# A kept score as two parts on two engines, and all sums on GpSimd, in the third feed-forward of a decoder stack

## The reference

```python
xn = _rmsnorm(x, norm_w)
q = (xn @ w_q.T).reshape(b, t, H, 2, DK)                    # H = 8 heads
sim1 = jnp.einsum('bthd,hkd->bthk', q[..., 0, :], keys[:, :, 0, :])   # 32 keys each
sim2 = jnp.einsum('bthd,hkd->bthk', q[..., 1, :], keys[:, :, 1, :])
s1, i1 = jax.lax.top_k(sim1, K)                             # K = 8
s2, i2 = jax.lax.top_k(sim2, K)
all_sc = (s1[..., :, None] + s2[..., None, :]).reshape(b, t, H, K * K)
fs, pk = jax.lax.top_k(all_sc, K)
...
hidden = jax.nn.gelu(jnp.einsum('btd,bthkd->bthk', xn, wd), approximate=False)
hidden = hidden * jax.nn.relu(fs)
return jnp.einsum('bthk,bthkd->btd', hidden, wu)
```

## Time and profile before

| | us |
|---|---|
| median of 3 runs | 3284.03 (3282.2 to 3285.31) |
| the profiled execution, its own time | 3292.13 |
| its span in the profile | 3290.0 |
| TensorE busy | 2657.0 (81%) |
| VectorE busy | 1842.7 (56%) |
| ScalarE busy | 1231.2 (37%) |
| GpSimd busy | 518.4 (16%) |

### The profile page before, as it was taken

One profiled execution on the slowest core, in us unless ns is written; L12 is line 12 of the kernel. 1 busy time (PEld: TensorE's weight loads), 2 busy tenths in 40 slices (PEclk: granted clock), 3 DMA queues, 4 the chain that ended last, 5 costly groups with the idle time before them and its releaser, 6 DMA issues.

```text
span 3290.0 us, 38345 instructions
## 1 busy us (share of the span) xinstructions
PE 2657.0 (81%) x13038; PEld 1292.2 (39%) x13089; DVE 1842.7 (56%) x4787; ACT 1231.2 (37%) x3064; POOL 518.4 (16%) x801
## 2 busy tenths in 40 slices
PE   6798898779987667888878988987899776678885
PEld 2233335334543543234423333452345335432353
DVE  5434438535655888624464444475257469875154
ACT  2545622453233101564334555224522231025741
POOL 1220001220112442000012200012201125410000
PEclk9988898889878778878769888898899687878776
DMA  4000000000100000000100000000001000000000
GB/s 164 2 1 1 1 1 25 25 2 20 33 13 0 0 26 26 1 1 30 36 8 2 1 1 1 1 25 26 1 20 33 13 1 0 26 27 1 1 1 7
DMA packets 16418, 49.52 MB, mean 15 GB/s; under 512 B 1761, under 2 KB 8801, under 8 KB 14434
## 3 DMA queue, kind: packets, MB, share of 16 engines
q1 hardware_dynamic: 15650, 45.79, 4.0%
q10 hardware_dynamic: 576, 1.29, 0.1%
HBM read 45.43 MB, written 1.05 MB: 14 GB/s over the span
## 4 chain that ended last, share of the span: by engine, by line
PE 60%; DVE 20%; ACT 9%; issue 7%; SPq 1%; POOL 1%; DMA 1%; ACTq 0%; DVEq 0%; POOLq 0%
PE psum L564 5%; PE psum L975 4%; PE psum L534 3%; DVE keep_s L2229 3%; PE psum L554 3%; PE psum L986 3%; PE psum L1510 2%; PE psum L1340 2%; PE psum L959 2%; PE psum L726 2%; DVE fs_v_s L2091 2%; ACT PT_s L630 2%; DVE mx_s L693 2%; PE psum L1802 2%; PE psum L801 2%
## 5 line engine op out<-in xcount | busy, mean ns | idle before, releaser
L630 ACT ACTIVATE PT_s<-psum 128x512 f32<-128x512 f32 (+3 forms) x768 | 342.3, 498 | 248.7 <-PE psum L554 246.0
L690 DVE CUSTOM_DVE_ANT_0 rest_s<-psum,packed_early 128x128 f32<-128x128 f32 (+3 forms) x512 | 226.6, 487 | 167.0 <-PE psum L540 164.8
L2134 PE MATMUL psum<-packed_early,keep_s 128*128 128x128 f32 x1024 | 177.7, 332 | 131.7 <-DVE keep_s L2229 131.4
L396 POOL TENSOR_SCALAR ve<-mv 128x4 f32<-128x4 f32 x48 | 14.4, 301 | 1691.0 <-DVE mv L386 1690.8
L554 PE MATMUL psum<-QS_s,KS_s 64*128 64x512 bf16 (+3 forms) x768 | 200.9, 366 | 55.8 <-DMA QS_s<-nmT_s 39.3
L540 PE MATMUL psum<-KS_s,QS_s 64*128 64x512 bf16 (+3 forms) x768 | 190.0, 364 | 54.0 <-DVE mx_s L693 29.4
L2091 POOL TENSOR_TENSOR buffer<-sim_s 128x1024 f32<-128x1024 f32 x80 | 187.3, 2353 | 240.6 <-DVE keep_s L2229 238.4
L564 PE MATMUL psum<-PT_s,vaug 128*9 128x512 f32 (+3 forms) x1536 | 183.5, 553 | 45.1 <-POOL PT_s L663 28.1
L2134 PEld LDWEIGHTS psum<-packed_early,keep_s 128*128 128x128 f32 x1024 | 147.4, 172 | 168.0 <-DVE keep_s L2229 155.9
L663 POOL TENSOR_SCALAR_AFFINE_SELECT PT_s<-PT_s 128x128 f32<-128x128 f32 x512 | 145.0, 293 | 387.7 <-ACT PT_s L630 382.8
L693 DVE TENSOR_REDUCE mx_s<-psum 128x1 f32<-128x512 f32 x256 | 160.5, 683 | 72.5 <-PE psum L540 72.1
(11 more groups left out here) (444 smaller groups left out, 5250.9 us busy)
## 6 DMA issues: line engine op xcount, KB each, us to landing
buffer<-packed_experts SPq DMA_DIRECT2D x36, 384.0 KB, 3.3
...
QS_s<-nmT_s SPq DMA_DIRECT2D x72, 8.0 KB
```

The lines of the kernel that those rows point to most:

```text
L630: a.activation(PT[:, u // 4 % 2, i, q0_of(c):T], bank[u % 3][:, q0_of(c):T], ACT.Exp, scale=scale).then_inc(exp_done.sem, 1)
L690: v.tensor_tensor_reduce(junk[:, u % 2, 0:w], bank[n % 4][:, 0:w], s.w["causal"][:, T - w:T], 1.0, -3e38, ALU.add, ALU.max, mx[:, j, h:h + ...
L2134: mm = pe.matmul(CT[:, c * P:(c + 1) * P], keep[:, n % KEPT, c * P:(c + 1) * P], s.w["ident"][:], is_transpose=True, start=(h == 0 and c % ...
```

## The change

A kept score is now written as two parts that add up to it: relu(sum - limit), made by ScalarE (L2194 of the changed kernel, into above), and limit x (sum >= limit), made by VectorE (`floored`, L2234 there, into floor) with one tensor_scalar that reads the limit twice as a pointer scalar. VectorE also makes the negated limits once a block (below, L2226 there), which ScalarE adds as a bias. TensorE transposes both parts into the same sums, 16 transposes a head instead of 8. GpSimd makes the sums of all eight heads (L2161 there), and VectorE none. above and floor have two buffers each (KEPT = 2) where keep had four. A buffer of sums is free when both parts have read it (risen, marked); the transposes wait for both parts as well.

```diff
-    KEPT, ON_POOL = 4, (0, 2, 4, 6, 7)
-    ON_DVE = tuple(h for h in range(NH) if h not in ON_POOL)
+    KEPT = 2
...
-                pe.wait_ge(*kept(n + 1))
+                pe.wait_ge(*risen(n + 1))
+                pe.wait_ge(*marked(n + 1))
...
-                for c in range(EC):
-                    mm = pe.matmul(CT[:, c * P:(c + 1) * P], keep[:, n % KEPT, c * P:(c + 1) * P], s.w["ident"][:], is_transpose=True,
-                                   start=(h == 0 and c % 4 == 0), stop=(h == NH - 1), skip_group_check=True)
+                for i, rows in enumerate((above, floor)):
+                    for c in range(EC):
+                        mm = pe.matmul(CT[:, c * P:(c + 1) * P], rows[:, n % KEPT, c * P:(c + 1) * P], s.w["ident"][:], is_transpose=True,
+                                       start=(h == 0 and i == 0 and c % 4 == 0), stop=(h == NH - 1 and i == 1), skip_group_check=True)
...
-            for i, h in enumerate(ON_POOL):
+            for h in range(NH):
                 yield max(13.0, at(j, h) - 3.0)
-                if i == 0:
+                if h == 0:
                     g.wait_ge(*sim_copied(j + 1))
-                n = j * len(ON_POOL) + i
+                n = j * NH + h
                 if n >= 2:
-                    m = n - 2
-                    g.wait_ge(*kept((m // len(ON_POOL)) * NH + ON_POOL[m % len(ON_POOL)] + 1))
-                sums(g, fs_g[:, n % 2], j, h).then_inc(sum_g.sem, 1)
+                    g.wait_ge(*risen(n - 1))
+                    g.wait_ge(*marked(n - 1))
+                m = sim[:, j % 2, h]
+                g.tensor_tensor(fs[:, n % 2], m[:, 0, :].unsqueeze(2).to_broadcast([P, NK, NK]),
+                                m[:, 1, :].unsqueeze(1).to_broadcast([P, NK, NK]), ALU.add).then_inc(summed.sem, 1)
...
+        for j in range(TJ):
+            for h in range(NH):
+                n = j * NH + h
+                yield at(j, h) + 0.4
+                total, ready = sum_of(n)
+                a.wait_ge(*ready)
+                if h == 0:
+                    a.wait_ge(*limits_ready(j + 1))
+                if n >= KEPT:
+                    a.wait_ge(*added(n - KEPT + 1))
+                a.activation(above[:, n % KEPT, :], total, ACT.Relu, bias=below[:, j % 2, h:h + 1]).then_inc(risen.sem, 1)
...
+            v.tensor_scalar(below[:, j % 2, :], thr[:, j % 2, :], -1.0, None, ALU.mult).then_inc(limits_ready.sem, 1)
...
             if n >= KEPT:
                 v.wait_ge(*added(n - KEPT + 1))
-            fs = fs.rearrange("p a b -> p (a b)")
-            v.scalar_tensor_tensor(keep[:, n % KEPT, :], fs, thr[:, j % 2, h:h + 1], fs, ALU.is_ge, ALU.mult).then_inc(kept.sem, 1)
+            v.tensor_scalar(floor[:, n % KEPT, :], total, thr[:, j % 2, h:h + 1], thr[:, j % 2, h:h + 1], ALU.is_ge, ALU.mult).then_inc(marked.sem, 1)
```

More of the change, by code:

```diff
@@ L2062, in l2_ffn @@
     N = TJ * NH
-    (chain, squares_ready, eps_added, inv_ready, xs_ready, xs_turned, xnT_ready, hidden_ready, gelu_ready, sim_ready, sim_copied, sum_v, sum_g,
-     kept, added, weighted, out_ready) = s.signals(
-        chain=1 + 4 * TJ, squares_ready=1, eps_added=1, inv_ready=1, xs_ready=TJ, xs_turned=1, xnT_ready=1, hidden_ready=EC, gelu_ready=EC,
-        sim_ready=TJ, sim_copied=TJ, sum_v=TJ * len(ON_DVE), sum_g=TJ * len(ON_POOL), kept=N, added=N, weighted=TJ, out_ready=TJ)
+    (chain, limits_ready, squares_ready, eps_added, inv_ready, xs_ready, xs_turned, xnT_ready, hidden_ready, gelu_ready, sim_ready, sim_copied, summed,
+     risen, marked, added, weighted, out_ready) = s.signals(
+        chain=1 + 4 * TJ, limits_ready=TJ, squares_ready=1, eps_added=1, inv_ready=1, xs_ready=TJ, xs_turned=1, xnT_ready=1, hidden_ready=EC, gelu_ready=EC,
+        sim_ready=TJ, sim_copied=TJ, summed=N, risen=N, marked=N, added=N, weighted=TJ, out_ready=TJ)
     s.new_stage()
@@ L2076, in l2_ffn @@
     thr = s.tile("thr9", [P, 2, NH])
-    fs_v = s.tile("fs_v9", [P, NK, NK])
-    fs_g = s.buffer[:, 2048:4096].rearrange("p (i a b) -> p i a b", i=2, a=NK)
-    keep = s.tile("keep9", [P, KEPT, NK * NK])
+    below = s.tile("below9", [P, 2, NH])
+    fs = s.buffer[:, 2048:4096].rearrange("p (i a b) -> p i a b", i=2, a=NK)
+    above = s.tile("above9", [P, KEPT, NK * NK])
+    floor = s.tile("floor9", [P, KEPT, NK * NK])
     cand = sq[:].rearrange("p j d -> p (j d)").rearrange("p (h a b) -> p h a b", h=NH, a=8)
@@ L2087, in at, with sum_of @@
         return T1 + D1 * (j * NH + h)
-    def sums(eng, dst, j, h):
-        m = sim[:, j % 2, h]
-        return eng.tensor_tensor(dst, m[:, 0, :].unsqueeze(2).to_broadcast([P, NK, NK]),
-                                 m[:, 1, :].unsqueeze(1).to_broadcast([P, NK, NK]), ALU.add)
+    def sum_of(n):
+        return fs[:, n % 2].rearrange("p a b -> p (a b)"), summed(n + 1)
     def tensor(pe):
@@ L2168, in copy_sim @@
             if j >= 2:
-                a.wait_ge(*kept(NH * (j - 1)))
+                a.wait_ge(*risen(NH * (j - 1)))
+                a.wait_ge(*marked(NH * (j - 1)))
             a.copy(sim[:, j % 2].rearrange("p h s n -> p (h s n)"), bank[2]).then_inc(sim_copied.sem, 1)
@@ L2179, in scalar @@
             a.activation(hid[:, c, :], bank[c % 2], ACT.Gelu).then_inc(gelu_ready.sem, 1)
-        for j in range(2, TJ):
-            yield at(j - 1, 1) + 3.0
-            copy_sim(j)
+        for j in range(TJ):
[9 more added lines that the diff above has]
+                a.activation(above[:, n % KEPT, :], total, ACT.Relu, bias=below[:, j % 2, h:h + 1]).then_inc(risen.sem, 1)
+                if h == 1 and 1 <= j < TJ - 1:
+                    yield at(j, h) + 3.0
+                    copy_sim(j + 1)
     def vector(v):
@@ L2210, in thresholds, with floored @@
             link(v.tensor_scalar(thr[:, j % 2, :], best[:, :, 7], 0.0, None, ALU.max))
-        def filtered(j, h):
+            v.tensor_scalar(below[:, j % 2, :], thr[:, j % 2, :], -1.0, None, ALU.mult).then_inc(limits_ready.sem, 1)
+        def floored(j, h):
             n = j * NH + h
-            if h in ON_DVE:
-                i = j * len(ON_DVE) + ON_DVE.index(h)
-                if i >= 1:
-                    before = i - 1
-                    v.wait_ge(*kept((before // len(ON_DVE)) * NH + ON_DVE[before % len(ON_DVE)] + 1))
-                sums(v, fs_v[:], j, h).then_inc(sum_v.sem, 1)
-                v.wait_ge(*sum_v(i + 1))
-                fs = fs_v[:]
-            else:
-                i = j * len(ON_POOL) + ON_POOL.index(h)
-                v.wait_ge(*sum_g(i + 1))
-                fs = fs_g[:, i % 2]
+            total, ready = sum_of(n)
+            v.wait_ge(*ready)
             if n >= KEPT:
                 v.wait_ge(*added(n - KEPT + 1))
-            fs = fs.rearrange("p a b -> p (a b)")
-            v.scalar_tensor_tensor(keep[:, n % KEPT, :], fs, thr[:, j % 2, h:h + 1], fs, ALU.is_ge, ALU.mult).then_inc(kept.sem, 1)
+            v.tensor_scalar(floor[:, n % KEPT, :], total, thr[:, j % 2, h:h + 1], thr[:, j % 2, h:h + 1], ALU.is_ge, ALU.mult).then_inc(marked.sem, 1)
         def weigh(j):
@@ L2244, in vector @@
                     weigh(j - 1)
-                filtered(j, h)
+                floored(j, h)
                 if h == 3 and j + 1 < TJ:
```

## The result

The changed kernel takes 3238.14 us (median of 4 runs, 3237.29 to 3253.97) and the kernel before, beside it, 3284.67 (3282.2 to 3290.74): a ratio of 0.9867, 95% interval 0.9834 to 0.9900. The forecast was 3282 with a range of 3250 to 3314, so the time is 44 us under the forecast and 12 under the range. The profiled execution has a span of 3236.6 us (3290.0 before) and its own time is 3238.3.

A forecast was written before the change was run, and what follows sets the result against it. The prediction took VectorE to bound B and TensorE's chain A, with C shared; after the change port and TensorE would limit B. 8 - 10 + 1 = -1 us a window, -2 in all, gave 3282 us from 3284.0, range 3250 to 3314.

The forecast's parts named there:

- A: Stage window's first part, 1028 to 1104 us, stream 1 still in context attention; TensorE's chain: +8 us (+3 to +14).
- C: Stage window's last part, 1196 to 1283 us, stream 1's last heads beside stream 0's next attention: +1 us (-6 to +9).
- B: Stage window's middle part, 1104 to 1196 us, both streams in the stage: from 92 to 82 us, -10.
- the sum of -1 us a window: Over each of the changed stage's two windows: 8 - 10 + 1 = -1 us, -2 in all.
- the port's rounds: In B, GpSimd and VectorE alternate on their shared port: 31 x (1.65 + 0.72) = 73.5 us.
- VectorE's relief: Filters and sums taken off VectorE: its chain share falls 4 to 5 us in A, 25 to 14 to 15 in C.
- a clock of 0.88: TensorE's granted clock assumed in B, up from 0.74, so that TensorE needs 75 us there.
- rival 2: TensorE becomes the bound, B's clock stays at 0.74: B -3, A +14, C +9, +20 a window, 3324 us; chance 0.20.
- Rival 1: The alone stretches absorb the second pass: A +3, C -6, B -14, -17 a window, 3250 us; chance 0.23.
- Rivals 3: VectorE's new operation runs at one element a cycle: B 0 to +2, +15 a window, 3314 us; chance 0.07.
- 4: GpSimd's sum takes 2.39 us, holding the port 2.14: no gain in B, +9 a window, 3302 us; chance 0.05.
- if A doesn't lengthen: Sign that the mechanism is wrong: A, forecast to go to about 84 us, does not get longer.

The follow-up runs named there:

- e3: The kernel before with all eight sums on GpSimd, the old filter and one transpose pass kept: 3253.7 us, ratio 0.9923.
- e7: e3 with each kept score also transposed twice and VectorE halving the sum as it weighs: 3277.9 us, ratio 0.9989.
- e5: The changed kernel with the limit's part made by scalar_tensor_tensor, the limit as second SBUF input, instead of the short tensor_scalar: 3284.3 us, ratio 1.0002.
- e2: The changed kernel without the transposes of floor, so the limit's part is missing in the result: 3200.5 us, ratio 0.9756.
- e1: The kernel before with each kept score transposed twice and VectorE halving the sum as it weighs: 3304.0 us, ratio 1.0082.
- e6: The changed kernel with three buffers instead of two for ScalarE's part: 3238.5 us, ratio 0.9882.
- e4: The changed kernel with the sums of heads 1, 3 and 5 back on VectorE, each just ahead of its own head's floor: 3272.2 us, ratio 0.9978.
- e9: The changed kernel with VectorE making the sums of heads 1, 3 and 5, each one head ahead: 3272.0 us, ratio 0.9952.

## Why the prediction was wrong

By the steps of the experiments, before to e3 to e7 to e5 to the changed kernel, a window's 21.6 us come apart as follows (the order matters: the second pass costs A 7.9 and C 4.9 beside the kernel before, 11.9 and 1.6 beside e3, and 6.9 and 8.5 beside e2):

| step | A | B | C | sum |
|---|---|---|---|---|
| all sums on GpSimd (e3 - before) | -5.0 | -3.0 | -8.2 | -16.2 |
| TensorE's second pass (e7 - e3) | +11.9 | +0.7 | +1.6 | +14.2 |
| ScalarE's part, two buffers (e5 - e7) | -0.5 | +0.5 | +0.9 | +0.9 |
| the short operation (changed - e5) | -5.6 | -15.1 | +0.2 | -20.5 |
| all | +0.8 | -16.9 | -5.5 | -21.6 |
| forecast | +8 | -10 | +1 | -1 |

The failed steps all lie in the sum of -1 us a window, and all three made the gain too small. In B too much was put on top of the port's rounds. In A and C the second pass and VectorE's relief were priced apart, as shares of one chain, and added.

*The bound of each stretch* was read half rightly. That the change gains in B and not in A held. In B the sum used the port, and that is the bound; that VectorE was 98% busy there was not the reason, since e3 takes twelve sums off it and gains 3.0 us. In A the chain was called TensorE's, and taking the sums off VectorE gave 5.0 us there.

*The prices of the parts* held: 0.81 us for the new operation, 1.15 for ScalarE's, 2.37 us a round worked out and 2.33 measured, and the new operation colliding like the old one. That ScalarE's part costs next to nothing held too.

*B, -10 forecast, -17 measured: the failed step is what was added to the port's rounds.* Between the cuts of the earlier trace rows the forecast had 73.5 us of rounds, 3.5 for candidate sums and limits, and 5 for block ends and short leads, 82 in all. Measured are 30 sums in 74 us: 69.9 us of rounds (30 x 2.33) and 4.1 for everything else, where 8.5 had been added; the rest of the miss is one head fewer between the cuts and 0.04 us a round. A block's end need not leave a gap. In the changed kernel, eleven sums of GpSimd follow one another from 1148.51 to 1174.04, and VectorE weighs a block (at 1153.96, 1.22 us) in their midst:

```profile
1148.51 25.53 POOL L2161 TENSOR_TENSOR buffer<-sim_s 128x1024 f32<-128x1024 f32 x11 [1.13 <-DVE floor_s L2234]
```

And TensorE was put at 75 us, through a clock of 0.88 taken from stretches where TensorE is 80 to 90% busy. The clock was 1.00, and TensorE busy 63 of 74 us. This estimate did not make the 82, which the port set, but it carried the risk. e1 shows the clock apart from the rest: the same B with 256 transposes more went from 0.74 to 0.91 and lost nothing. The same step carried rival 2 (3324, 0.20), which had B at 0.74 with twice the transposes. The risk was priced backwards, since the clock rose with the work that was to suffer from it.

*A, +8 forecast, +1 measured: the failed step is the adding of two prices, each taken from one chain.* The second pass was put at 11 to 13, VectorE's relief at 4 to 5, its part of the one chain that ended last. In the order of the table the pass is 11.9, and the relief is what was mis-sized: 5.0 for the sums and 5.6 for the short operation. In the order before, e1, e7 both terms were: the pass costs 7.9, and the relief is 6.6 (1.0 and 5.6). No order that was measured gives 12 and 4. TensorE's busy time, forecast at 71 to 77 us, came to 65, its clock going from 0.87 to 0.96. VectorE was 14.6 us less busy in A in the end (52.7 to 38.1), and 10.6 came back. A share of one chain is a poor price for taking work off. The likely reason is that, with two streams woven together, the other stream's chain leads through the same engine; no run shows that apart. Part of A's second 5.6 us may be the clock: A's length times its granted clock is 69.9 us in e5 (78.5 x 0.89), 68.7 in e7 and 69.3 in the changed kernel, as if TensorE had one amount of work and only its clock differed. But e1 has 72.8 (80.0 x 0.91) with the same transposes. This is read off profiles and was not tested.

*C, +1 forecast, -5.5 measured: the failed term is the second pass.* It was put at 10.8 us, the transposes' share of the chain paid once more. It costs 4.9 beside the kernel before and 1.6 once the sums are gone. The relief was put at 10 and is 8.0. (The forecast's working for it doesn't come out either: 12 heads at 0.72 and 0.4 are 13.4 us, not 14 to 15, and it doesn't say why 12 of the stretch's 17 heads.) In C either of the two alone is enough to hold the end: with one pass and the long filter 71.5 (e3), two passes and the long operation 74.0 (e5), two passes and the short one 74.2, one pass and the short one 65.7 (e2). So there the two prices don't add. This is what one finds where the longer of two paths counts, and I had added both.

*The rivals.* Rival 1, "the alone stretches absorb the second pass", named the right direction in all three stretches (A +3, B -14, C -6, -17 a window) and fell short only by 5 us a window; it had 0.23. Rivals 3 (one element a cycle) and 4 (a sum at 2.39 alone) are refuted by 811 ns and by the minimum of 1902 ns. The rule named there, of GpSimd's ratio for the fp32 add ("GPSIMD Engine Reference", section "Elementwise — side-by-side cycle accounting", in the Trainium skill), advises against what e3 shows to gain 26 us: GpSimd's 1.90 us a sum are slower than VectorE's 1.21, but VectorE was what the stage waited for. The Trainium skill's rule on the port ("SBUF — State Buffer", section "Who interferes with whom") held in the main: the trace agrees that the two alternate. It doesn't have them shut each other out for the whole of both recorded lengths: a round is 2.33 us, and the operations alone are 1.90 and 0.81, 2.71 together.

*What was named as proof against the mechanism*: "if A doesn't lengthen". Between the same instructions A is 0.8 us longer, which by that sign says that the sum was wrong, and it was. The other two signs were to be B keeping its 92 us, and VectorE waiting for ScalarE's half; neither is there. (B has 74 us, and the third buffer of e6 changes nothing.) Over the whole span VectorE's part stands idle for 6.1 us, nearly all of it for TensorE (changed kernel):

```profile
L2234 DVE TENSOR_SCALAR floor_s<-buffer,thr_s 128x1024 f32<-128x1024 f32 x128 | 158.4, 1271 | 6.1 <-PE psum L2135 5.1 <-POOL buffer L2161 0.7
```

Still open: which of A's two terms was off, since that depends on the order; why C in e4 is 10 us longer than in the changed kernel, why A in e9 is 4 longer than in e4, and how much of A's relief is the clock's.
